# Attention's weights inverted in quarters of rows on 128 partitions, spread by DMA

## The chip, the cores and the metric

One core of a Trainium2 chip runs the whole kernel. The metric is the device time of one execution in microseconds (us), the median of several runs. One further execution was recorded by the profiler; every row below comes from it.

## The reference, cut to what matters

A macaron layer: half a feed-forward step, an attention-like mixer, half a feed-forward step. The batch is B = 4 sequences of T = 512 tokens and D = 512. The part that the change touches is the mixer's weights p_w and its normalisation; K = 32 heads of H = 8 channels, each with M = 8 phases.

```python
x = x + 0.5 * ffn(layernorm(x))            # top 2 of 8 experts, and a shared one
x = x + mixer(layernorm(x))                # the lines below
x = x + 0.5 * ffn(layernorm(x))            # the same weights

z = causal_conv4(layernorm(x) @ W_mem)     # in mixer: 256 values k_val, 32 scores s_raw
log_p = clip(score_scale * s_raw, -20, 20)
p_w = exp(log_p + log_w)                   # [b, l, K]
phi = k_val[..., None] * theta             # [b, l, K, H, M]
cs = cumsum([p_w, p_w * cos(phi), p_w * sin(phi)], axis=1)
den, num_re, num_im = split(cs)
inv_den = 1 / max(den, 0.0001)
state = (num_re + i num_im) * inv_den
out = sum over M of state * conj(q)        # q = x @ W_q
y = (y_val * silu(y_gate)) @ W_out         # from out, per head
```

## The kernel before, in words

All engines work from orders that a list planner writes when the program is built. `piece(engine, stage, cost, *after)` (L273 on) names a stage of a batch with its counted cost and what it comes after; `orders()` (L457) lets every engine in turn take the open piece with the longest way to the end, and the pieces of the phase steps on DVE yield to all others. On the chip each engine runs its list strictly in order, with semaphore waits. The planner's times are counts, the chip's are the trace's.

There are eight feed-forward jobs (four batches before attention, four after), each two a group: four groups of 23 blocks of expert rows, whose results are added to DRAM one block after another. Attention runs batch by batch between them: batches 0 and 1 when group 0 has been added, batches 2 and 3 when group 1 has. Jobs 4 and 5 read attention's batches 0 and 1, jobs 6 and 7 batches 2 and 3; group 3's blocks come last.

The head of attention's batch b (`plan_head`, L375):

- `a_mem` (PE, then DVE `convolve`, L1278): first the 32 rows of scores, then two tiles of k_val, 128 x 512 each.
- `a_p`: `log_weights` (L1292) on DVE, then `weights` (L1028) on ACT, the exp: p, 32 partitions (the heads) x 512 tokens, in `low_rows`.
- `a_fall`: `falls` (L1311), DVE: a reciprocal of p (L1316), then p of the token before times it (L1318). That is the factor by which the running sum falls from token to token, since the kernel scans sums already divided by p.
- `a_den`: `denominators` (L1320), DVE: a scan for the sums (L1324), the floor of 1e-4 (L1326), a reciprocal (L1328) and the fraction p / den (L1330), all 32 x 512. `s_row`, into which the scan writes, also holds the next batch's scores.
- `a_spread`: for each half, PE's `spread_falls` (L837) copies each head's row of falls to the head's 8 partitions by a matmul with a 0/1 matrix, and ACT's `keep_falls` (L1032) copies it from PSUM to `pwx`. Half 1 of `pwx` is read until the last scan of the batch before.
- `a_q`: four tiles of queries, which SP stores to DRAM (`store_query`, L1696).

Then 16 steps (`plan_step`, L413), n = 0 to 15, eight to a half. DVE makes the phases (`c_turn`, L1342 and L1344), ACT their sine and cosine (L1043 to L1046), DVE scans both (`c_scan`, L1355, reads `pwx`), multiplies them by the queries (`c_times`, L1362, L1367) and adds (`c_sum`, L1378 to L1388). SP loads the queries of a step (`load_query`, L1704) as soon as the step two before it has been summed. After step 7 and step 15 comes `c_out`: PE spreads the fractions (`spread_inverse`, L843), DVE scales (L1400), SP moves the result (`move_output`, L1718), and then the gates and the rows of the output follow on PE, ACT, DVE and POOL (`plan_tail`, L426).

DMAs of the head, the steps and the tail all are issued by SP, in one order. A job's input rows are fetched by SP too (`load_rows`, L1666); job 3's go into the buffer of batch 0's queries and wait for all four stores of them.

Of the kernel before, what the change touches and what calls it, by code (L numbers as in the profile page):

```python
# [9 lines left out]
F32 = mybir.dt.float32  # L10
# [5 lines left out]
P = 128  # L16
# [45 lines left out]
def macaron(nc, x, small, gate_w, sw1, sw2, b2_rows, w_experts, w_mem, w_q, w_bd, w_out, out):  # L62
# [32 lines left out]
    with ctx:  # L95
# [13 lines left out]
        pw, logw_sb = (low_rows[0:K, :, :], low_rows[2 * K:3 * K, :, :]), low_rows[K:2 * K, 0, :]  # L109
        w_all = sb("w_all", [P, E * WE])  # L110
# [121 lines left out]
        q_dram = nc.dram_tensor("q_cols", (2, KQ, M, HH, 2, T), F32)  # L232
        slots_dram = [nc.dram_tensor(f"slots{g}", (P * NB, 2), F32).ap() for g in range(NG)]
# [141 lines left out]
        def plan_head(b):  # L375
# [31 lines left out]
            for half in range(HALVES):  # L407
                s = ("a_spread", b, half)
                piece("PE", s, 1.2, ("DVE", ("a_fall", b)),
                      *([("DVE", ("c_scan", b - 1, half * M + M - 1))] if b else []), bank=[("misc", ("ACT", s))])  # L410
                piece("ACT", s, 0.6, ("PE", s))

        def plan_step(i):  # L413
# [6 lines left out]
            piece("DVE", ("c_scan", b, n), 2.5, ("ACT", ("c_turn", b, n)), ("ACT", ("a_spread", b, half)),  # L420
# [5 lines left out]
        def plan_tail(b):  # L426
# [3 lines left out]
            for half in range(HALVES):  # L430
# [5 lines left out]
                piece("PE", s, 1.3, ("DVE", ("a_den", b)), ("DVE", ("c_scan", b, half * M + M - 1)), *free,  # L436
# [123 lines left out]
        spread_p = signal("s_spread_p", staged("a_spread", "PE"))  # L560
# [19 lines left out]
        pwx_made = signal("s_pwx", staged("a_spread", "ACT"))  # L580
# [16 lines left out]
        den_made = signal("s_den", [(b, i) for b in range(B) for i in range(4)])  # L597
# [31 lines left out]
        a_loaded = [signal(f"s_a_loaded{tb}", range(B), 16) for tb in range(TB)]  # L629
        q_stored = [signal(f"s_q_stored{q}", range(B), 16) for q in range(KQ)]  # L630
# [24 lines left out]
        for s in ORDER:  # L655
# [24 lines left out]
            elif s[0] == "a_spread":  # L680
                misc_uses.append((s, pwx_made.at(s[1:])))
# [14 lines left out]
        def tensor_program():  # L696
# [140 lines left out]
            def spread_falls(b, half):  # L837
# [72 lines left out]
        def scalar_program():  # L910
# [121 lines left out]
            def keep_falls(b, half):  # L1032
                bank = misc_turn.at["a_spread", b, half][0]
                act.wait_ge(*spread_p.at((b, half)))
                if b > 0:
                    act.wait_ge(*scanned.at((b - 1, half * M + M - 1)))
# [839 lines left out]
```

## Time and profile before

| what | us |
|---|---|
| median of 3 runs | 1338.7 |
| lowest and highest | 1325.69, 1348.18 |
| the profiled execution, its own time | 1340.56 |
| its span, first to last instruction | 1339.3 |
| busy: PE, DVE, ACT, POOL | 1047.6, 731.5, 593.6, 439.6 |

The busy share of an engine is an average over stages with different limits, so the rows below go by stretch and by instruction. Times in rows are us from the span's start unless marked ns; PE is the tensor engine, DVE the vector engine, ACT the scalar engine, POOL GpSimd, SP the sync engine, and SPq its DMA queue.

### The profile page before, as it was taken

What the parts mean: (1) busy time and instruction counts of PE and PEld (TensorE: products, weight loads), DVE (VectorE), ACT (ScalarE), POOL (GpSimd) and SP (SyncE); (2) the same over time, 40 slices, a digit from 0 to 9 for tenths busy, and PEclk for the clock granted to TensorE, in tenths of its full rate; (3) what the DMA queues carried; (4) which work ended last, traced back from release to release, by engine and by line L of the source; (5) the groups of instructions that cost most, each with busy time, mean ns of one, the idle gap of its engine ahead of it and who ended that gap; (6) DMA issues with size and microseconds to landing.
All of it is one profiled execution on the core that took longest, in us unless ns stands there. A gap on an engine that the chain in (4) does not pass through costs nothing.

```text
span 1339.3 us, 10709 instructions
## 1 busy us (share of the span) xinstructions
PE 1047.6 (78%) x3296; PEld 574.9 (43%) x3296; DVE 731.5 (55%) x1130; ACT 593.6 (44%) x1008; POOL 439.6 (33%) x429
## 2 busy tenths in 40 slices
PE   5998888982978878968938287867977698969884
PEld 3545555332534444444313142344444443536552
DVE  3311000067879898979999885978988520200000
ACT  3423433233425888557323333357666541314332
POOL 4153443202553353331000246032452212154442
PEclk8998999995989989979968587989988899779887
DMA  8954554424144675773344624265685425034544
GB/s 284 332 171 87 94 95 79 79 58 134 36 98 109 173 143 117 160 196 93 94 111 87 206 56 93 60 179 112 134 215 108 68 37 112 32 64 95 94 85 56
DMA packets 60204, 155.15 MB, mean 116 GB/s; under 512 B 10578, under 2 KB 10578, under 8 KB 57974
## 3 DMA queue, kind: packets, MB, share of 16 engines
q0 software_dynamic: 29568, 60.90, 26.9%
q1 hardware_dynamic: 30582, 93.58, 22.6%
q8 instruction: 28, 0.46, 0.1%
q14 instruction: 26, 0.21, 0.1%
HBM read 99.74 MB, written 58.88 MB: 118 GB/s over the span
## 4 chain that ended last, share of the span: by engine, by line
DMA 33%; PE 27%; DVE 12%; POOL 10%; ACT 8%; issue 8%; SPq 1%; POOLq 0%; ACTq 0%; DVEq 0%
DMA x_rows<-ys,into_i 14%; DMA out_rows<-ys,into_i 10%; PE misc L867 6%; POOL slots L1538 6%; PE hps L736 5%; DMA xs<-x_normal,rows_i 4%; PE yps L805 3%; PE hps L789 3%; PE yps L748 2%; PE xps L719 2%; DVE run L1355 2%; ACT ys L975 2%; DMA xin<-in_x 1%; DMA xin<-x_rows 1%; ACT xin L996 1%
## 5 line engine op out<-in xcount | busy, mean ns | idle before, releaser
L805 PE MATMUL yps<-w_all,hidden_sb 128*128 x368 | 209.5, 700 | 55.8 <-ACT hidden_sb L962 55.0
L789 PE MATMUL hps<-w_all,hidden_sb 128*128 x736 | 188.2, 403 | 8.5 <-ACT hidden_sb L945 8.5
L1355 DVE TENSOR_TENSOR_SCAN run<-pwx,trig 128x512 f32<-128x512 f32 x128 | 149.5, 1210 | 46.0 <-ACT trig L1046 45.2
L789 PEld LDWEIGHTS hps<-w_all,hidden_sb 128*128 128x128 f32 x736 | 148.3, 207 | 54.3 <-issue 36.3
L1550 POOL DMA_INDIRECT xs<-x_normal,rows_i x92 | 106.1, 1153 | 139.2 <-PE xps L780 119.9
L975 ACT ACTIVATE ys<-yps,slots 128x512 f32<-128x512 f32 x92 | 63.1, 686 | 169.8 <-PE yps L805 62.3
L1563 POOL DMA_INDIRECT out_rows<-ys,into_i x46 | 77.5, 1685 | 166.5 <-ACT ys L975 94.2
L805 PEld LDWEIGHTS yps<-w_all,hidden_sb 128*128 128x128 f32 x368 | 74.3, 214 | 131.8 <-issue 129.8
L736 PE MATMUL hps<-xnT,sw_sb 128*128 128x512 f32 x256 | 129.9, 662 | 0.8 <-ACT xnT L919 0.8
L1563 POOL DMA_INDIRECT x_rows<-ys,into_i x46 | 77.8, 1691 | 153.9 <-DMA x_rows<-ys,into_i 85.0
L748 PE MATMUL yps<-sw_sb,hidden_sb 128*128 128x512 f32 x256 | 124.0, 629 | 0.0
L780 PE MATMUL xps<-ident,xs 128*128 128x128 f32 x368 | 59.9, 294 | 63.2 <-DMA xs<-x_normal,rows_i 54.8
L1538 POOL DMA_INDIRECT slots<-told,dest_i x64 | 79.7, 1245 | 64.6 <-DVE cmp_a L1225 32.5
L867 PE MATMUL misc<-turns_sb,tail_sb 128*128 128x512 f32 x192 | 88.8, 616 | 6.5 <-DVE tail_sb L1416 6.5
L710 PE MATMUL xps<-ident,xin 128*128 128x128 f32 x128 | 25.3, 353 | 74.8 <-ACT xin L996 68.8
L780 PEld LDWEIGHTS xps<-ident,xs 128*128 128x128 f32 x368 | 46.1, 151 | 83.3 <-DMA xs<-x_normal,rows_i 56.6
L736 PEld LDWEIGHTS hps<-xnT,sw_sb 128*128 128x128 f32 x256 | 53.3, 214 | 66.4 <-issue 65.9
L1362 DVE TENSOR_TENSOR trig<-run,qx 128x1024 f32<-128x1024 f32 x64 | 78.2, 1221 | 4.8 <-DMA qx<-q_cols 4.5
L1271 DVE BATCH_NORM_STATS2 stats_attn<-xin 128x6 f32<-128x512 f32 x16 | 10.5, 690 | 125.6 <-DMA xin<-x_rows 125.6
L1367 DVE TENSOR_TENSOR qx<-run,qx 128x1024 f32<-128x1024 f32 x64 | 78.0, 1219 | 0.0
L748 PEld LDWEIGHTS yps<-sw_sb,hidden_sb 128*128 128x128 f32 x256 | 48.2, 199 | 57.5 <-issue 57.5
L1043 ACT ACTIVATE trig<-trig 128x512 f32<-128x512 f32 x64 | 40.3, 630 | 71.1 <-DVE trig L1344 68.2
(199 smaller groups left out, 1587.4 us busy)
## 6 DMA issues: line engine op xcount, KB each, us to landing
qx<-q_cols SPq DMA_DIRECT2D x128, 256.0 KB
x_normal<-xin SPq DMA_DIRECT2D x32, 256.0 KB
w_all<-in_w_experts SPq DMA_DIRECT2D x8, 1024.0 KB, 8.3
xin<-x_rows SPq DMA_DIRECT2D x32, 256.0 KB, 4.7
turns_sb<-in_w_out SPq DMA_DIRECT2D x3, 1536.0 KB
xin<-in_x SPq DMA_DIRECT2D x16, 256.0 KB, 3.8
x_rows<-ys POOLq DMA_DIRECT2D x16, 256.0 KB
q_cols<-xin SPq DMA_DIRECT2D x16, 256.0 KB
```

The costliest lines, as they stand in the source:

```text
L736: t = PE.matmul(hps[:, bank, :], sw1_sb[:, c, n * P:(n + 1) * P], xnT[:, c, :], start=c == 0, stop=c == KC - 1)
L748: t = PE.matmul(yps[:, bank, :], hT[:, n, tb * P:(tb + 1) * P], sw2_sb[:, n, :], start=False, stop=n == SC - 1)
L780: t = PE.transpose(xps[:, bank, c * P:(c + 1) * P], xs[:, j % NX, c * P:(c + 1) * P], ident[:, :])
L789: t = PE.matmul(hps[:, bank, 0:H], xT[:, j % 2, c, :], w_all[:, bass.ds(expert[j] + c * H, H)], start=c == 0, stop=c == KC - 1)
L805: t = PE.matmul(yps[:, bank, :], hb[:, j % 2, ec, :], w_all[:, bass.ds(expert[j] + (KC * H + ec * D), D)], start=ec == 0, stop=ec == EC - 1)
L867: t = PE.matmul(misc[:, bank, :], yT[:, v, tb * P:(tb + 1) * P], wout_sb[:, v, :], start=v == 0, stop=v == VT - 1)
L975: SE.activation(ys[:, j % 2, :], yps[:, bank, :], ACT.Copy, scale=slots[:, g % 2, j, 1:2]).then_inc(*ys_kept.of((g, j)))
L1355: t = VE.tensor_tensor_scan(run[:, c, :], pwx[:, n // M, :], trig[:, n % 2, c, :], 0.0, ALU.mult, ALU.add)
L1362: VE.tensor_tensor(trig[:, n % 2, :, :], run[:, :, :], qx[:, n % NQX, :, :], ALU.mult).then_inc(*real_made.of((b, n)))
L1538: GE.indirect_dma_start(slots_dram[g], bass.IndirectOffsetOnAxis(dest_i[:, g % 2, t, r:r + 1], 0), told[:, g % 2, t, r, :], None).then_inc ...
L1550: GE.indirect_dma_start(xs[:, j % NX, :], None, xn_rows[g % 2], bass.IndirectOffsetOnAxis(rows_i[:, g % 2, j:j + 1], 0)).then_inc(*xs_load ...
L1563: GE.indirect_dma_start(INTO[g], bass.IndirectOffsetOnAxis(into_i[:, g % 2, j:j + 1], 0), ys[:, j % 2, :], None, compute_op=ALU.add).then_ ...
```

## The change

Falls and fractions are computed on all 128 partitions, each holding a quarter (128 tokens) of a head's row. ACT's exp still writes p on 32 partitions. SP stores p to DRAM, one element past the start of `u_dram`, and loads it back twice in quarters: from element 1 (`u_q`) and from element 0 (`fall_q`, the weights of the token before). DVE's `falls` works on these 128 x 128 tiles, SP stores the result, and one DMA for each half reads a head's row eight times over into `pwx`. The matmuls and the ACT copies of `a_spread` go. DVE scans the sums on 32 partitions as before, now straight after the exp; they make the same trip through DRAM, `fractions` works on quarters, and the result goes back through DRAM to `pw`. The planner counts these DMAs 2.4 us (2.8 for the spreads) past their issue. Cut to its core:

```diff
+        quarter_rows = sb("quarter_rows", [P, 3, T // 4])
+        u_q, fall_q, den_q = [quarter_rows[:, i, :] for i in range(3)]
...
                 free = [("DVE", ("c_turn", b - 2, i * M + M - 1))] if i < HALVES and b >= 2 else []
-                free += [("DVE", ("a_den", b - 1))] if i == HALVES and b else []
+                free += [("SP", ("a_den", b - 1, 0), 2.4)] if i == HALVES and b else []
                 piece("PE", s, 4.1, *kept_rows, weights, *free, *before, bank=[("misc", ("DVE", s))])
                 piece("DVE", s, 3.0, ("PE", s))
                 before = [("PE", s)]
             piece("DVE", ("a_p", b), 3.1, ("DVE", ("a_mem", b, HALVES)),
-                  *([("PE", ("c_out", b - 2, HALVES - 1)), ("PE", ("a_spread", b - 2, HALVES - 1))] if b >= 2 else []))
+                  *([("PE", ("c_out", b - 2, HALVES - 1))] if b >= 2 else []))
             piece("ACT", ("a_p", b), 0.7, ("DVE", ("a_p", b)), table="exp")
-            piece("DVE", ("a_fall", b), 4.0, ("ACT", ("a_p", b)))
-            piece("DVE", ("a_den", b), 5.8, ("DVE", ("a_fall", b)))
+            piece("SP", ("a_p", b, 0), 0.5, ("ACT", ("a_p", b)))
+            piece("SP", ("a_p", b, 1), 0.9, ("SP", ("a_p", b, 0), 2.4), *([("DVE", ("a_frac", b - 1))] if b else []))
+            piece("DVE", ("a_fall", b), 1.4, ("SP", ("a_p", b, 1), 2.4))
+            piece("SP", ("a_fall", b), 0.5, ("DVE", ("a_fall", b)))
+            piece("DVE", ("a_den", b), 1.4, ("ACT", ("a_p", b)))
+            piece("SP", ("a_den", b, 0), 0.5, ("DVE", ("a_den", b)))
+            piece("SP", ("a_den", b, 1), 0.5, ("SP", ("a_den", b, 0), 2.4))
+            piece("DVE", ("a_frac", b), 1.8, ("SP", ("a_den", b, 1), 2.4), ("SP", ("a_p", b, 1), 2.4))
+            piece("SP", ("a_frac", b, 0), 0.5, ("DVE", ("a_frac", b)))
+            piece("SP", ("a_frac", b, 1), 0.5, ("SP", ("a_frac", b, 0), 2.4))
...
                 s = ("a_spread", b, half)
-                piece("PE", s, 1.2, ("DVE", ("a_fall", b)),
-                      *([("DVE", ("c_scan", b - 1, half * M + M - 1))] if b else []), bank=[("misc", ("ACT", s))])
-                piece("ACT", s, 0.6, ("PE", s))
+                piece("SP", s, 0.5, ("SP", ("a_fall", b), 2.4),
+                      *([("DVE", ("c_scan", b - 1, half * M + M - 1))] if b else []))
...
-            piece("DVE", ("c_scan", b, n), 2.5, ("ACT", ("c_turn", b, n)), ("ACT", ("a_spread", b, half)),
+            piece("DVE", ("c_scan", b, n), 2.5, ("ACT", ("c_turn", b, n)), ("SP", ("a_spread", b, half), 2.8),
...
-                piece("PE", s, 1.3, ("DVE", ("a_den", b)), ("DVE", ("c_scan", b, half * M + M - 1)), *free,
+                piece("PE", s, 1.3, ("SP", ("a_frac", b, 1), 2.4), ("DVE", ("c_scan", b, half * M + M - 1)), *free,
...
             def falls(b):
-                p, fall = pw[b % 2][:, 0, :], pw[b % 2][:, 1, :]
+                vec.wait_ge(*u_loaded.at((b, 1)))
+                if b > 0:
+                    vec.wait_ge(*falls_stored.at(b - 1))
+                VE.reciprocal(den_q, u_q).then_inc(*falling.of((b, 0)))
+                vec.wait_ge(*falling.at((b, 0)))
+                VE.tensor_tensor(fall_q, fall_q, den_q, ALU.mult).then_inc(*falling.of((b, 1)))
+
+            def denominators(b):
+
+                none = zero1[b % 2 * 2 * K:(b % 2 * 2 + 1) * K, 0:1].broadcast_to([K, T])
                 vec.wait_ge(*p_made.at(b))
-                VE.reciprocal(fall, p).then_inc(*falling.of((b, 0)))
-                vec.wait_ge(*falling.at((b, 0)))
-                VE.tensor_tensor(fall[:, 1:T], p[:, 0:T - 1], fall[:, 1:T], ALU.mult).then_inc(*falling.of((b, 1)))
-
-            def denominators(b):
-
-                p, den = pw[b % 2][:, 0, :], s_row
-                none = zero1[b % 2 * 2 * K:(b % 2 * 2 + 1) * K, 0:1].broadcast_to([K, T])
-                VE.tensor_tensor_scan(den, p, none, 0.0, ALU.add, ALU.add).then_inc(*den_made.of((b, 0)))
-                vec.wait_ge(*den_made.at((b, 0)))
-                VE.tensor_scalar(den, den, 1e-4, None, ALU.max).then_inc(*den_made.of((b, 1)))
-                vec.wait_ge(*den_made.at((b, 1)))
-                VE.reciprocal(den, den).then_inc(*den_made.of((b, 2)))
-                vec.wait_ge(*den_made.at((b, 2)))
-                VE.tensor_tensor(p, p, den, ALU.mult).then_inc(*den_made.of((b, 3)))
-
-                vec.wait_ge(*den_made.at((b, 3)))
+                VE.tensor_tensor_scan(s_row, pw[b % 2][:, 0, :], none, 0.0, ALU.add, ALU.add).then_inc(*den_made.of(b))
+
+            def fractions(b):
+
+                vec.wait_ge(*den_loaded.at(b))
+                VE.tensor_scalar(den_q, den_q, 1e-4, None, ALU.max).then_inc(*part_made.of((b, 0)))
+                vec.wait_ge(*part_made.at((b, 0)))
+                VE.reciprocal(den_q, den_q).then_inc(*part_made.of((b, 1)))
+                vec.wait_ge(*part_made.at((b, 1)))
+                VE.tensor_tensor(den_q, u_q, den_q, ALU.mult).then_inc(*part_made.of((b, 2)))
...
-                vec.wait_ge(*pwx_made.at((b, n // M)))
+                vec.wait_ge(*falls_loaded[n // M].at(b))
...
+            def move_weights(b, part):
+                if part == 0:
+                    sp.wait_ge(*p_made.at(b))
+                    if b >= 2:
+                        sp.wait_ge(*u_loaded.at((b - 2, 1)))
+                    SP.dma_start(whole_rows(u_dram[b % 2], 1), pw[b % 2][:, 0, :]).then_inc(*u_stored.of(b))
+                else:
+                    sp.wait_ge(*u_stored.at(b))
+                    sp.wait_ge(*before_first.at(1))
+                    if b > 0:
+                        sp.wait_ge(*part_made.at((b - 1, 2)))
+                        sp.wait_ge(*falls_stored.at(b - 1))
+                    SP.dma_start(u_q, quarters(u_dram[b % 2], 1)).then_inc(*u_loaded.of((b, 0)))
+                    SP.dma_start(fall_q, quarters(u_dram[b % 2])).then_inc(*u_loaded.of((b, 1)))
+            def store_falls(b):
+                sp.wait_ge(*falling.at((b, 1)))
+                if b >= 2:
+                    for half in range(HALVES):
+                        sp.wait_ge(*falls_loaded[half].at(b - 2))
+                SP.dma_start(quarters(falls_dram[b % 2]), fall_q).then_inc(*falls_stored.of(b))
+            def spread_falls(b, half):
+                sp.wait_ge(*falls_stored.at(b))
+                if b > 0:
+                    sp.wait_ge(*scanned.at((b - 1, half * M + M - 1)))
+                src = bass.AP(falls_dram[b % 2].tensor, falls_dram[b % 2].offset + half * KT * T,
+                              [[T, KT], [0, HH], [1, T]])
+                SP.dma_start(pwx[:, half, :], src).then_inc(*falls_loaded[half].of(b))
+            def move_sums(b, part):
+                if part == 0:
+                    sp.wait_ge(*den_made.at(b))
+                    if b >= 2:
+                        sp.wait_ge(*den_loaded.at(b - 2))
+                    SP.dma_start(whole_rows(den_dram[b % 2]), s_row).then_inc(*den_stored.of(b))
+                else:
+                    sp.wait_ge(*den_stored.at(b))
+                    sp.wait_ge(*falling.at((b, 1)))
+                    SP.dma_start(den_q, quarters(den_dram[b % 2])).then_inc(*den_loaded.of(b))
+            def move_fractions(b, part):
+                if part == 0:
+                    sp.wait_ge(*part_made.at((b, 2)))
+                    if b >= 2:
+                        sp.wait_ge(*part_loaded.at(b - 2))
+                    SP.dma_start(quarters(part_dram[b % 2]), den_q).then_inc(*part_stored.of(b))
+                else:
+                    sp.wait_ge(*part_stored.at(b))
+                    sp.wait_ge(*den_made.at(b))
+                    sp.wait_ge(*u_stored.at(b))
+                    SP.dma_start(pw[b % 2][:, 0, :], whole_rows(part_dram[b % 2])).then_inc(*part_loaded.of(b))
...
+                    for i in range(2):
+                        SP.dma_start(u_dram[i][0:1, :], xs[0:1, i, 0:1]).then_inc(*before_first.of(i))
```

## Rows read from the trace of the kernel before

**Rows 1.** Busy time of each engine by stretch, with granted PE clock, DMA share, GB/s.

```profile
650.00:700.00 50.00, 27.06 (x61) 10.68 (x59) 48.72 (x56) 14.49 (x22) 2.59 (x3) 0.78 0.43 107
...
1250.00:1300.00 50.00, 42.60 (x158) 26.86 (x158) 0.00 (x0) 18.26 (x44) 21.93 (x17) 0.90 0.51 90
```

**Rows 2.** The chain that ended last, batch 2's head: start, us, what.

```profile
661.66 3.25 DVE low_rows L1316
...
669.60 3.35 DVE low_rows L1328
```

**Rows 3.** The same chain, batch 3's head.

```profile
849.17 3.35 DVE low_rows L1316
...
856.26 3.35 DVE low_rows L1328
...
861.80 1.21 PE misc L840 x2
...
872.35 7.51 DMA xs<-x_normal,rows_i
```

**Rows 4.** The same chain, batch 0's head.

```profile
287.45 3.26 DVE low_rows L1316
...
296.31 0.51 SPq L1701
...
296.86 14.10 DMA xin<-in_x
```

**Rows 5.** The same chain, batch 1's second spread.

```profile
509.84 1.05 PE misc L840 x2
```

**Rows 6.** DVE's groups by line and form: busy us, mean ns; idle before, releaser.

```profile
L1328 DVE RECIPROCAL low_rows<-low_rows 32x512 f32<-32x512 f32 x4 | 13.4, 3342 | 0.1
L1316 DVE RECIPROCAL low_rows<-low_rows 32x512 f32<-32x512 f32 x4 | 13.3, 3337 | 0.1
...
L1324 DVE TENSOR_TENSOR_SCAN low_rows<-low_rows,zero 32x512 f32<-32x512 f32 x4 | 4.9, 1214 | 0.1
...
L1330 DVE TENSOR_TENSOR low_rows<-low_rows 32x512 f32<-32x512 f32 x4 | 2.7, 680 | 0.1
...
L1326 DVE TENSOR_SCALAR low_rows<-low_rows 32x512 f32<-32x512 f32 x4 | 1.7, 416 | 0.1
...
L1161 DVE RECIPROCAL gr<-diff 128x4 f32<-128x4 f32 x8 | 1.4, 178 | 0.3
...
L1211 DVE TENSOR_TENSOR pair<-sel,dest 128x128 f32<-128x128 f32 x4 | 1.2, 293 | 0.1
```

**Rows 7.** DMA issues: count, KB each, median us from issue to landing.

```profile
xin<-x_rows SPq DMA_DIRECT2D x32, 256.0 KB, 4.7
...
slots<-slots SPq DMA_DIRECT2D x4, 23.0 KB, 3.4
```

**Rows 8.** The chain of waits: the last of four DMAs of `move_output`, batches 1 and 2.

```profile
696.35 3.65 DMA outT<-tail_sb
...
1000.11 8.30 DMA outT<-tail_sb
```

**Rows 9.** DVE in order of time: start, us, what, idle before.

```profile
301.43 2.34 DVE L1355 TENSOR_TENSOR_SCAN run<-pwx,trig 128x512 f32<-128x512 f32 x2
...
310.99 2.67 DVE L1110 BATCH_NORM_STATS2 stats_ffn<-xin 128x6 f32<-128x512 f32 x4 [3.78 <-DMA xin<-in_x]
...
362.19 2.33 DVE L1355 TENSOR_TENSOR_SCAN run<-pwx,trig 128x512 f32<-128x512 f32 x2
...
370.32 2.33 DVE L1355 TENSOR_TENSOR_SCAN run<-pwx,trig 128x512 f32<-128x512 f32 x2
```

**Rows 10.** ACT in order of time, batch 0's exp.

```profile
283.57 0.63 ACT L1030 ACTIVATE low_rows<-low_rows 32x512 f32<-32x512 f32 x1 [0.77 <-DVE low_rows L1309]
```

**Rows 11.** Who waited for whom: us in total, times, longest us.

```profile
DVE run L1355 <- ACT trig L1046: 45.2, 15, 6.1
```

**Rows 12.** The same of SP's queue.

```profile
SPq L1716 <- DVE outT L1388: 320.0, 39, 25.2
```

**Rows 13.** SP's queue in order of time, `load_tail_weights` of batch 1.

```profile
669.85 0.33 SPq L1734 DMA_DIRECT2D turns_sb<-in_w_out  x1
```

More of the change, by code:

```diff
@@ L232, in macaron, with quarters, whole_rows @@
         q_dram = nc.dram_tensor("q_cols", (2, KQ, M, HH, 2, T), F32)
+        u_dram = [nc.dram_tensor(f"weights{i}", (K * T + 1, 1), F32).ap() for i in range(2)]
+        falls_dram = [nc.dram_tensor(f"falls{i}", (K, T), F32).ap() for i in range(2)]
+        den_dram = [nc.dram_tensor(f"sums{i}", (K, T), F32).ap() for i in range(2)]
+        part_dram = [nc.dram_tensor(f"fractions{i}", (K, T), F32).ap() for i in range(2)]
+        def quarters(dram, start=0):
+            return bass.AP(dram.tensor, dram.offset + start, [[T // 4, P], [1, T // 4]])
+        def whole_rows(dram, start=0):
+            return bass.AP(dram.tensor, dram.offset + start, [[T, K], [1, T]])
         slots_dram = [nc.dram_tensor(f"slots{g}", (P * NB, 2), F32).ap() for g in range(NG)]
@@ L596, in macaron @@
         falling = signal("s_falling", [(b, i) for b in range(B) for i in range(2)])
-        den_made = signal("s_den", [(b, i) for b in range(B) for i in range(4)])
+        den_made = signal("s_den", range(B))
+        part_made = signal("s_part", [(b, i) for b in range(B) for i in range(3)])
         phase_int = signal("s_phase_int", staged("c_turn", "DVE"))
@@ L629, in macaron @@
         a_loaded = [signal(f"s_a_loaded{tb}", range(B), 16) for tb in range(TB)]
+        u_stored = signal("s_u_stored", range(B), 16)
+        u_loaded = signal("s_u_loaded", [(b, i) for b in range(B) for i in range(2)], 16)
+        falls_stored = signal("s_falls_stored", range(B), 16)
+        falls_loaded = [signal(f"s_falls_loaded{half}", range(B), 16) for half in range(HALVES)]
+        den_stored = signal("s_den_stored", range(B), 16)
+        den_loaded = signal("s_den_loaded", range(B), 16)
+        part_stored = signal("s_part_stored", range(B), 16)
+        part_loaded = signal("s_part_loaded", range(B), 16)
+        before_first = signal("s_before_first", range(2), 16)
         q_stored = [signal(f"s_q_stored{q}", range(B), 16) for q in range(KQ)]
@@ L1030, in weights @@
                 SE.activation(pw[b % 2][:, 0, :], pw[b % 2][:, 0, :], ACT.Exp).then_inc(*p_made.of(b))
[L1032 to L1036, printed above, removed]
-                SE.copy(pwx[:, half, :], misc[:, bank, :]).then_inc(*pwx_made.of((b, half)))
             def waves(b, n):
@@ L1285, in convolve @@
                     vec.wait_ge(*phase_made.at((b - 2, i * M + M - 1)))
+                if i == HALVES and b:
+                    vec.wait_ge(*den_stored.at(b - 1))
                 VE.tensor_scalar(o, z, conv_sb[at, i, CW - 1:CW], None, ALU.mult).then_inc(*convolved.of((b, i, 0)))
@@ L1480, in vector_program @@
                     denominators(*at)
+                elif stage == "a_frac":
+                    fractions(*at)
                 elif stage == "c_turn":
@@ L1786, in sync_program @@
                     store_query(*at)
+                elif stage == "a_p":
+                    move_weights(*at)
+                elif stage == "a_fall":
+                    store_falls(*at)
+                elif stage == "a_spread":
+                    spread_falls(*at)
+                elif stage == "a_den":
+                    move_sums(*at)
+                elif stage == "a_frac":
+                    move_fractions(*at)
                 elif stage == "c_query":
```

17 lines of the change are left out of this document (1 added, 16 removed).

## The prediction

> **What bounds the kernel now.** I read the busy times by stretch first. Ahead of attention and behind it DVE stands still (0 of 50 us at 1250 [rows 1]) and the adding of expert blocks sets the time; between some 300 and 1060 us DVE is the engine that is nearly full (48.7 of 50 us at 650 [rows 1]). Averages over the span (DVE 55%) hide that. Then the chain of waits, which shows where the head of a batch is on the path. Batch 2: both reciprocals on the chain [rows 2]. Batch 3: both again, behind them the two matmuls of a spread (1.21 us), and through PE's order the next block's rows [rows 3]. Batch 0: the falls' reciprocal, which holds up the first phases, through them the query tile that ACT copies behind their sines, its store, and job 3's rows [rows 4]. Batch 1: of its head only a spread [rows 5]; its arithmetic is beside the path, since blocks of group 1 set the pace there. Last the waits: DVE loses 45.2 us at 15 scans to ACT's late sines [rows 11], so a DVE that is faster elsewhere partly waits there instead.
>
> **DVE's work.** Before, a batch costs 3.34 + 3.34 (reciprocals) + 2 x 0.68 (multiplies) + 1.21 (scan) + 0.42 (floor) = 9.67 us [rows 6]. A reciprocal takes 3342 ns at 512 elements a partition and 178 at 4, so 6.23 ns an element, whether on 32 or 128 partitions; at 128 elements that gives 178 + 124 x 6.23 = 950 ns. A multiply of 128 x 128 stands in the rows (0.29) [rows 6]. The floor is between 0.18 and 0.29; I take 0.24. After: 2 x 0.95 + 2 x 0.29 + 1.21 + 0.24 = 3.93 us. The gain is 5.74 us a batch, 23 us of DVE's work in all; on the path only for batches 2 and 3.
>
> **PE and ACT.** 16 matmuls (8 spreads) and 8 ACT copies go. On the path stand 1.21 us for batch 3 and 1.05 us for batch 1 [rows 3, 5]; I count these 2.26 us as won, the rest at nothing, as DVE's or the blocks' waits cover it.
>
> **The new round trips.** No row shows a 64 KB DMA through DRAM. Call L the time from issue to landing. From below: 3.4 us for 23 KB [rows 7]. From above: 8.3 us, the slower of two moves of 128 KB within SBUF; the other took 3.65 [rows 8]. I take 3.65, which is nearest to the small DMAs' median, and keep 3.4 and 8.3 for the range. An issue costs SP some 0.55 us (0.51 in [rows 4]).
>
> The exp to `falls`: store (0.55 + L), then two loads (1.1 + L): 2L + 1.65 = 8.95 us. DVE's order is fixed, so `falls` waits there with all phase steps queued behind it, for whatever the planner has not filled. It counts this trip 0.1 + 0.5 + 2.5 + 0.9 + 2.5 = 6.5 us and lets DVE finish a piece of up to 2.5. A step that it counts 9.1 (1.3 + 2.5 + 2.5 + 2.8) takes 8.13 us, from scan to scan [rows 9], so this cover is worth 0.89 of its count: 5.8 us, with half a piece 6.9. A stall of 2.05 us is left.
>
> The sums to `fractions`: the load waits for `falling`, since `den_q` is the falls' scratch, but the planner doesn't list that wait. It may put `fractions` right behind `falls`, or one piece later. The load takes 0.55 + 3.65 = 4.2 us behind the falls; between no cover and 2.3 us of it I take the middle, 1.15: a stall of some 3.05 us. Together the stalls are 3L - 5.85, or 5.1 us a batch against 5.74 won; they are equal at L = 3.86 us.
>
> The way of the falls into `pwx` (one store, two spreads) and of the fractions back (two DMAs) has cover. Batch b's first scan comes many steps after its head for b = 1 to 3, and the fractions are read after step 7, seven steps of 8.13 us later. SP gets ten more DMAs a batch (some 5.5 us) with four waits for landings between them. Its queue stood idle for 320 us waiting for DVE's sums before it could load queries [rows 12]; a load is wanted one step after it may go, so holding SP up by some 4 us (8.13 less an issue pair and a landing of 3 to 4) costs nothing, two trips in a row would. I cost that at 0 and keep it in the slow rival. Two 4-byte stores at the start lie beside the first weights' loads: 0.
>
> The Trainium skill, "DMA: Bandwidth & Descriptors", section "Anatomy of one DMA — SWDGE (gpsimd) path", fits a DMA at about 2.0 us plus bytes over 436 GB/s. By it a 64 KB trip would be an estimated 2.15 us (this queue is another than the one it was fitted on), the stalls 0.6 us a batch and the sum near the fast rival; the 3.4 us row stands against it.
>
> **Batch 0.** The exp ends at 284.20 [rows 10]. Quarters loaded at 293.15, falls at 294.4, stored at 298.6, spread (256 KB, 4.7 us [rows 7]) at 303.85: the first scan is 2.4 us later than the 301.43 of before, less than the 3.78 us that DVE idled just after for job 3's rows [rows 9]. Against it the first phases start up to 3.9 us earlier (reciprocal and multiply gone from ahead of them), and job 3's rows with them, if SP isn't holding for falls just then; the falls' store lands 2.3 us after the 296.31 at which the last query store went [rows 4]. Between -3.9 and +2.4 I take -1.
>
> **Sum.** Batch 0 -1; batch 1 -1.05; batch 2 5.1 - 5.74 = -0.6; batch 3 the same and -1.21, -1.8. Together -4.5 us on the profiled execution's 1340.56, 1336.1. That execution is 1.86 above the median of the runs shown; so 1334 us, to compare with 1338.7. The arithmetic is won, and nearly all of it given back as waits for landings.
>
> **The rivals.**
> 1. The trips are covered, as the planner means them to be. The whole 5.74 comes through twice, batch 0 gives 3.9, the spreads 2.26: -17.6, or 1321 us. For it: DVE's pieces come in lumps, and a stall at `falls` lets ACT catch up on sines it would have been waited for anyway (45.2 us [rows 11]). Against it: 3.4 us is the shortest landing in the rows, and the planner counts 2.4. The skill's fit, above, would give this case.
> 2. Small DMAs land late, behind larger ones on SP's queue. The place is DVE's two in-order waits. At L = 8.3 each batch stalls 19.05, +13.3 for batch 2 and +12.1 for batch 3; batch 0's first scan slips by four trips x 4.65 = 18.6 more, less the idle left, +17; with batch 1, +41, or 1380 us. It decides from L = 3.86, and passes 2% slower near L = 6.9. For it: query loads of 2 x 256 KB and a load of 1.5 MB at 669.85 [rows 13] are issued by SP within 10 us of batch 2's head. Against it: only one of the moves seen took that long.
>    The skill, same page, section "Queues, rings and completion order", says that each DMA engine takes descriptors in ring order. By this a small DMA stands behind the query loads ahead of it; the 3.65 and the 8.3 agree with it without showing it.
> 3. The orders of all engines are planned anew, since costs and pieces changed. That moves blocks, sines and table loads against one another without anything in the change meaning it. Half of the 45.2 us of waits for sines gained or lost is 22 us either way: 1312 or 1356.
> 4. It doesn't take DVE's time down: a reciprocal on 128 partitions costs by some other count. The equal per-element rate of 32 x 512 and of 128 x 4 speaks against it; with no gain and these stalls, +8: 1348. Small.
>
> **How the numbers follow.** Forecast 0.5, own range 1325 to 1346. Rival 1 0.17, rival 2 0.13, rival 3 0.17, rival 4 0.03. The range is 1312 to 1364: below, rival 3's fast end beyond rival 1; above, rival 2 up to L of about 6.8. A measurement of this kernel tells 2%, 27 us, from no change (below 1312, above 1365). Faster by that needs rival 1 and luck of order together: 0.10. Slower needs rival 2 well past its point, or a bad order with stalls: 0.16. Within: 0.74.
>
> **What would show it.** Right: reciprocals of 128 x 128 at 0.9 to 1.0 us; DVE's busy time down by 23 us; idle ahead of the falls' reciprocal and of the floor on quarters, released by DMAs from `weights` and `sums`, some 20 us in all over four batches; batch 0's first scan at 302 to 306. Wrong: no idle there and a span below 1325 (rival 1); over 8 us idle at either in a batch, or scans waiting for queries (rival 2); the stalls as told but blocks and sines in other places with tens of us between them (rival 3).

## The result, and the profile after

The changed kernel takes 1328.25 us (median of 18 runs, 1318.9 to 1340.46) against 1336.69 us for the kernel before on the same chips (18 runs, 1325.69 to 1348.18): ratio 0.9929, 95% interval 0.9904 to 0.9954. By the medians that is 8.4 us faster, clear of the noise and well within 2%. A ratio is estimated from the single runs, so it can differ from the quotient of the two medians, here by up to 0.3%. The forecast was 1334 us, 4.5 us of gain, with a range of 1312 to 1364. The profiled execution has a span of 1325.1 us against 1339.3.

First the engines' busy times, from the page of the changed kernel.

```profile
PE 1021.4 (77%) x3280; PEld 564.0 (43%) x3280; DVE 708.5 (53%) x1130; ACT 594.9 (45%) x1005; POOL 448.8 (34%) x429
```

DVE's busy time is down by 23.0 us from 731.5. The groups by line and form show the same instructions on quarters, to be held against [rows 6]:

```profile
L1343 DVE RECIPROCAL quarter_rows<-quarter_rows 128x128 f32<-128x128 f32 x4 | 3.8, 952 | 0.1
L1328 DVE RECIPROCAL quarter_rows<-quarter_rows 128x128 f32<-128x128 f32 x4 | 3.8, 950 | 11.4 <-DMA quarter_rows<-weights 11.4
...
L1330 DVE TENSOR_TENSOR quarter_rows<-quarter_rows 128x128 f32<-128x128 f32 x4 | 1.2, 292 | 0.1
...
L1341 DVE TENSOR_SCALAR quarter_rows<-quarter_rows 128x128 f32<-128x128 f32 x4 | 0.9, 226 | 7.6 <-DMA quarter_rows<-sums 7.6
```

Read the part behind the bar (busy us, mean ns of one; idle us just before, with what ended it): the falls' reciprocal (L1328) stood 11.4 us waiting for its quarters, the floor (L1341) 7.6 us for the sums. Of 23 us of work won, 19.0 us come back as waits. The four batches differ; DVE in order of time, batches 0 and 1:

```profile
299.05 0.95 DVE L1328 RECIPROCAL quarter_rows<-quarter_rows 128x128 f32<-128x128 f32 x1 [10.12 <-DMA quarter_rows<-weights]
...
304.37 0.23 DVE L1341 TENSOR_SCALAR quarter_rows<-quarter_rows 128x128 f32<-128x128 f32 x1 [1.03 <-DMA quarter_rows<-sums]
...
394.70 0.95 DVE L1328 RECIPROCAL quarter_rows<-quarter_rows 128x128 f32<-128x128 f32 x1 [0.69 <-DMA quarter_rows<-weights]
...
400.18 0.23 DVE L1341 TENSOR_SCALAR quarter_rows<-quarter_rows 128x128 f32<-128x128 f32 x1 [4.20 <-DMA quarter_rows<-sums]
```

Batch 2 waits 0 and 1.89 us, batch 3 0.62 and 0.49. These are not DVE's only new waits. Over the whole span, the changed kernel's multiplies wait 11.2 us for loads of queries, against 4.5 before, while its scans wait 27.5 us for sines, against 45.2 [rows 11]:

```profile
DVE run L1368 <- ACT trig L1059: 27.5, 12, 8.5
...
DVE trig L1375 <- DMA qx<-q_cols: 11.2, 2, 6.5
```

The queries' wait of before:

```profile
DVE trig L1362 <- DMA qx<-q_cols: 4.5, 2, 3.8
```

So where does the 14.2 us between the two profiled executions come from? Instructions that both traces have cut the span into stretches. A first sum is DVE's first addition of a half's first step (`c_sum`, steps 0 and 8), a scaling is its `scale_output`, behind steps 7 and 15:

| stretch | before | after | difference |
|---|---|---|---|
| start to attention's first rows | 250.83 | 249.53 | -1.3 |
| from there to the first sum of batch 3's step 8 | 733.80 | 736.97 | +3.2 |
| from there to the scaling after step 15 | 81.89 | 67.73 | -14.2 |
| from there to the end | 272.8 | 270.9 | -1.9 |

All four heads, with all that the change touches, lie in the second stretch, and there the changed kernel is not faster. How far to trust the rows: in a second trace of the changed kernel, the run e_after_again below, the second stretch takes 746.9 us and the third 67.7. So the +3.2 is less than two executions of one kernel differ by, and the -14.2 is far more. The gain is in batch 3's last eight steps, in which DVE has the same work as before. Busy times of that stretch (us: PE, PEld, DVE, ACT, POOL, granted PE clock, DMA share, GB/s), before and after:

```profile
984.63:1066.52 81.89, 57.75 (x181) 34.05 (x182) 59.05 (x76) 51.94 (x87) 24.94 (x23) 0.83 0.53 109
```

```profile
986.50:1054.23 67.73, 51.26 (x175) 30.77 (x174) 58.96 (x76) 51.03 (x83) 28.93 (x21) 0.90 0.58 126
```

DVE runs the same 76 instructions in 59.0 us in both. Who kept it waiting in that stretch (us in total, times, longest us), before and then after:

```profile
DVE run L1355 <- ACT trig L1046: 16.2, 4, 6.1
DVE tail_sb L1412 <- ACT tail_sb L1056: 4.2, 2, 2.4
DVE tail_sb L1400 <- PE misc L846: 2.1, 1, 2.1
```

```profile
DVE run L1368 <- ACT trig L1059: 4.6, 1, 4.6
DVE tail_sb L1425 <- ACT tail_sb L1069: 2.2, 2, 1.3
DVE tail_sb L1413 <- PE misc L868: 1.5, 1, 1.5
```

DVE waits 22.5 us before and 8.3 after: the 14.2 us. PE's granted clock is 0.90 after against 0.83, each a mean between its two levels of 1.2 and 2.4 GHz; PE stood idle for 16.5 us of the stretch after, for 24.1 before. The shorter stretch comes with the higher clock; no run separates the two. The planner has put the block work of group 2 and the sines in another order. One more wait there is ACT's. It copies each block's rows into one of two `ys` buffers, and must wait until the add of the block two before has landed in DRAM:

```profile
ACT ys L975 <- DMA out_rows<-ys,into_i: 14.3, 4, 6.2
```

That is before; after, ACT has no such wait in the stretch. So rival 3 has to be tested against the forecast's own reasons.

### The profile page after: what moved, and what is told of

It is laid out like the page before. It is cut to its first block, busy times and chain, and to the rows that moved or that the text cites. A ratio compares the mean times of both kernels' runs of the same rounds, so it can differ in the third digit from the quotient of the medians.

```text
span 1325.1 us, 10725 instructions
## 1 busy us (share of the span) xinstructions
PE 1021.4 (77%) x3280; PEld 564.0 (43%) x3280; DVE 708.5 (53%) x1130; ACT 594.9 (45%) x1005; POOL 448.8 (34%) x429
## 4 chain that ended last, share of the span: by engine, by line
DMA 35%; PE 26%; ACT 11%; POOL 10%; DVE 10%; issue 8%; SPq 1%; POOLq 0%; ACTq 0%; DVEq 0%
DMA x_rows<-ys,into_i 12%; DMA out_rows<-ys,into_i 10%; POOL slots L1553 6%; PE hps L764 5%; PE misc L889 4%; DMA xs<-x_normal,rows_i 4%; PE yps L833 4%; PE hps L817 3%; DMA xin<-x_rows 2%; PE xps L747 2%; DVE run L1368 2%; ACT ys L995 2%; PE misc L852 2%; PE yps L776 2%; ACT L982 1%
## 5 line engine op out<-in xcount | busy, mean ns | idle before, releaser
L833 PE MATMUL yps<-w_all,hidden_sb 128*128 x368 | 191.2, 646 | 49.5 <-ACT hidden_sb L982 48.8
L817 PE MATMUL hps<-w_all,hidden_sb 128*128 x736 | 192.2, 409 | 9.4 <-ACT hidden_sb L965 9.1
L1368 DVE TENSOR_TENSOR_SCAN run<-pwx,trig 128x512 f32<-128x512 f32 x128 | 149.3, 1207 | 30.2 <-ACT trig L1059 27.5
L1578 POOL DMA_INDIRECT out_rows<-ys,into_i x46 | 80.7, 1754 | 155.6 <-ACT ys L995 73.9
L1578 POOL DMA_INDIRECT x_rows<-ys,into_i x46 | 80.6, 1752 | 151.8 <-DMA x_rows<-ys,into_i 93.4
L833 PEld LDWEIGHTS yps<-w_all,hidden_sb 128*128 128x128 f32 x368 | 70.3, 202 | 118.8 <-issue 116.5
L776 PE MATMUL yps<-sw_sb,hidden_sb 128*128 128x512 f32 x256 | 120.0, 612 | 0.0
L1553 POOL DMA_INDIRECT slots<-told,dest_i x64 | 76.2, 1191 | 72.8 <-DVE cmp_a L1236 37.8
L889 PE MATMUL misc<-turns_sb,tail_sb 128*128 128x512 f32 x192 | 92.4, 637 | 10.7 <-DVE tail_sb L1429 10.7
L1375 DVE TENSOR_TENSOR trig<-run,qx 128x1024 f32<-128x1024 f32 x64 | 78.0, 1219 | 11.4 <-DMA qx<-q_cols 11.2
```

The lines of the kernel that those rows point to most:

```text
L776: t = PE.matmul(yps[:, bank, :], hT[:, n, tb * P:(tb + 1) * P], sw2_sb[:, n, :], start=False, stop=n == SC - 1)
L817: t = PE.matmul(hps[:, bank, 0:H], xT[:, j % 2, c, :], w_all[:, bass.ds(expert[j] + c * H, H)], start=c == 0, stop=c == KC - 1)
L833: t = PE.matmul(yps[:, bank, :], hb[:, j % 2, ec, :], w_all[:, bass.ds(expert[j] + (KC * H + ec * D), D)], start=ec == 0, stop=ec == EC - 1)
L889: t = PE.matmul(misc[:, bank, :], yT[:, v, tb * P:(tb + 1) * P], wout_sb[:, v, :], start=v == 0, stop=v == VT - 1)
L1368: t = VE.tensor_tensor_scan(run[:, c, :], pwx[:, n // M, :], trig[:, n % 2, c, :], 0.0, ALU.mult, ALU.add)
L1375: VE.tensor_tensor(trig[:, n % 2, :, :], run[:, :, :], qx[:, n % NQX, :, :], ALU.mult).then_inc(*real_made.of((b, n)))
```

## The experiments

Theory A is the forecast's: DVE's arithmetic in the heads is on the path, and is mostly given back as waits for landings. Theory B is rival 3: the gain is the order that the planner wrote for the new pieces. The experiments fall into three groups, on chips 14, 10 and 14. Each ratio is to the kernel before in the same group (medians 1336.73, 1330.06 and 1340.77 us).

**Less arithmetic, old order.** The kernel before, with falls and fractions cut to 128 of 512 columns. The rest of the falls is left at zero (a tile `short`), so its output is another one:

```diff
-                VE.reciprocal(fall, p).then_inc(*falling.of((b, 0)))
+                VE.reciprocal(fall[:, 1:P + 1], p[:, 1:P + 1]).then_inc(*falling.of((b, 0)))
...
-                VE.reciprocal(den, den).then_inc(*den_made.of((b, 2)))
+                VE.reciprocal(den[:, 0:P], den[:, 0:P]).then_inc(*den_made.of((b, 2)))
```

> The kernel before, in its own order and with PE's spreads, but the falls' reciprocal and multiply and the fractions' floor, reciprocal and multiply work on 128 of 512 columns (falls are 0 for the other tokens, and the falls' tile stands in for the fractions in the second spread, so the mixer's output is another one). DVE loses 5.7 us a batch, nothing waits for a trip. Theory A (arithmetic on the path): batches 2 and 3 give 5.7 each and batch 0 up to 3.9, so 11 to 15 us faster than before, ratio 0.989 to 0.992. Theory B (the gain is the new order, the arithmetic is covered): within 4 us of before, ratio 0.997 to 1.0.

Measured: 1331.52 us, ratio 0.9966 (0.9937 to 0.9995), just below Theory B's range and well short of Theory A's. Its trace says where. From attention's first rows to the first sum of batch 3's step 8 it takes 726.1 us against 733.8, 7.7 less. Cut at the first sum of each half of a batch, the stretch that holds batch 2's head takes 95.7 us and batch 3's 109.6. Three traces of the old work in the old order up to there (the kernel before, and the runs e_late_order and e_sines_ahead below) have 101.2 to 102.8 and 115.7 to 116.8. So these two are some 6 us shorter, where the cut removes 5.8 us of DVE each. Batch 1's is not shorter (123.7 against 121.4 to 123.1). The last eight steps take 85.7 us instead of 81.9. In the old order the arithmetic reaches the path where Theory A has it, but only some 5 us of it are left at the end of the kernel.

**The arithmetic back, new order.** The changed kernel with spare reciprocals behind each wait:

```diff
+                vec.wait_ge(*spared.at(4 * b + 0))
+                VE.reciprocal(spare[:, 0:200], spare[:, 0:200]).then_inc(*spared.of(4 * b + 1))
...
                 VE.reciprocal(den_q, u_q).then_inc(*falling.of((b, 0)))
```

> The changed kernel in its own order; inside `falls` two more reciprocals of 128 x 200 and inside `fractions` two of 128 x 215, behind the waits, so that DVE has its 5.7 us a batch back. Theory A: 11 us slower than the changed kernel for batches 2 and 3, so ratio to before 0.999 to 1.003. Theory B: at most 4 us slower than the changed kernel, ratio 0.993 to 0.996.

Measured: 1345.47 us, ratio 1.0065 (1.0033 to 1.0097), 1.4% slower than the changed kernel by the two ratios: 18 us (13 to 24, by the intervals) for 23 us of DVE work. That is outside both ranges, and more than Theory A's 11. Where the time goes is not shown. Three traces have the changed work in the new order up to batch 3's step 8 (the changed kernel twice, and e_late_old below), and take 737.0, 743.9 and 746.9 us from attention's first rows to there; with the spare work it is 757.8. The stretch with batch 1's head takes 120.8 us against 115.3 to 120.0, batch 2's 112.7 against 109.5 to 113.6, batch 3's 114.6 against 108.3 to 115.2. Each lies within 1 us of the longest of the three. The one that stands out holds no head: from batch 1's first sum to that of its step 8, 91.4 us against 84.5 to 86.9.

**The two orders exchanged.** In both kernels the planner's lists were replaced after planning. Here is the edit that puts the changed kernel's work in the old order, shortened and with comments added:

```diff
-        ORDERS = orders()
+        ORDERS, ENDED = orders()          # with the plan of before
+        ORDERS = old_order()              # the new pieces put in by time
```

> The changed kernel's work, but PE, ACT, DVE, POOL and SP keep the order of the kernel before for all that both have; the sums' scan stands where the falls stood, the falls where the denominators stood, the fractions a step later, the new DMAs of SP between by time. Theory A: about the changed kernel's time or some us less, since the falls have more cover, ratio 0.989 to 0.994. Theory B: as the kernel before, ratio 0.998 to 1.002.

> The kernel before's work (32 partitions, PE's spreads), in the order that the changed kernel's planner writes; the old denominators stand where the fractions stand, the spreads on PE and ACT go in by time. Theory A: no faster than before, ratio 0.998 to 1.003 (1334 to 1341 us). Theory B: as the changed kernel, ratio 0.991 to 0.995.

Measured, with the two kernels themselves, as ratios:

| | old order | new order |
|---|---|---|
| old work | 1 | 0.9928 (0.9897 to 0.9958) |
| new work | 1.0119 (1.0071 to 1.0167) | 0.9929 (0.9904 to 0.9954) |

The old arithmetic on 32 partitions, with PE's spreads, gains in the new order just what the changed kernel gains. Theory B holds: in one and the same order, the new work and the old differ by 0 us, give or take 5. In the old order the new work costs 1.2%, which neither theory had. The order written by hand around it has less cover, as DVE's waits of that kernel show:

```profile
DVE quarter_rows L1359 <- DMA quarter_rows<-sums: 24.4, 4, 9.5
```

Another 13.9 us go to the weights: 38.3 us of waits against 19.0. So part of that 1.2% is likely my placing of the new pieces, not the old order as such.

The kernel with the old work in the new order also shows what the new DMAs do to the queries. Without them, DVE's waits over the whole span are:

```profile
DVE run L1386 <- ACT trig L1077: 40.6, 14, 9.5
...
DVE trig L1393 <- DMA qx<-q_cols: 0.2, 1, 0.2
```

With the new work, in the same order, the queries' wait is 11.2 us and the sines' 27.5. So the changed kernel wins 23 us of DVE's work and 13 us of waits for sines, and pays 19 us at the trips, 11 us for late queries and 2 us at batch 0's first scan (waits of one trace each). That is some 4 us, and the two kernels' times are equal within 5.

**Only the late order.** The plan of before for what it starts ahead of batch 3's step 8, the plan of after from there:

```diff
+        limit = ENDED["DVE", ("c_scan", 3, 8)] - 2.5
+        for engine, stages in ORDERS.items():
+            early = [k for k in stages if ENDED[engine, k] - old_work[engine, k][0] < limit]
+            late = [k for k in later[engine] if k not in early and (engine, k) in old_work]
+            ORDERS[engine] = early + late
```

> The kernel before's work; every engine keeps the order of before for what the plan starts ahead of the scan of batch 3's step 8, and from there on takes the order of the changed kernel's plan. Theory B1 (the gain is the order of the last eight steps and the output of batch 3): as fast as the whole new order, ratio 0.990 to 0.994, with some 68 us from step 8's first sum to the second scaling instead of 82. Theory B2 (the new order gains all along): half the gain or less, ratio 0.996 to 1.0.

Measured: 0.9901 (0.9867 to 0.9936), in Theory B1's range. Its last eight steps, in busy times by stretch:

```profile
980.41:1048.24 67.83, 52.08 (x175) 31.65 (x176) 58.88 (x76) 51.22 (x84) 29.26 (x22) 0.90 0.57 128
```

And the reverse on the changed kernel, beside the changed kernel itself:

> The changed kernel's work and its own order up to the scan of batch 3's step 8, and from there on the order of the kernel before. If the order of the last eight steps is where the changed kernel's gain comes from, it loses all of it: some 82 us instead of 68 from step 8's first sum to the second scaling, ratio 0.999 to 1.006. If the arithmetic or the order ahead of it brings the gain, ratio 0.991 to 0.996.

> The changed kernel itself, as the reference of this chip for the three below: ratio 0.990 to 0.995.

Measured: 1.0023 (0.9996 to 1.0051) with the old late order, 0.9914 (0.9882 to 0.9946) for the changed kernel on that chip.

```profile
995.72:1076.72 81.00, 55.56 (x180) 32.60 (x178) 59.02 (x75) 51.33 (x85) 26.21 (x23) 0.83 0.53 108
```

Either kernel takes 68 us with the new late order and 81 to 82 with the old, and has the gain or doesn't. This is shown from both sides. In all traces of this case, the eight with the new late order take 65.7 to 69.0 us there, the four with the old one 81.0 to 85.7.

**A plan that differs for no reason.** One number of the planner in the kernel before:

```diff
-        HOP = 0.1
+        HOP = 0.15
```

> The kernel before with one number of the planner changed (the step between engines counted 0.15 us instead of 0.1), so the same work in an order that differs about as much as the changed kernel's does, meant for nothing. If any new order moves the time by a per cent either way (theory B), the ratio lies outside 0.996 to 1.004, on either side. If orders of this kind are worth little (theory A), it lies within.

Measured: 0.9936 (0.9907 to 0.9964). A new plan meant for nothing is worth about as much as the change. Its last eight steps take 77.4 us, 4.5 less than before, so the rest of its gain comes from elsewhere.

**What in the late order.** ACT's list alone, in the kernel before:

```diff
+        line = ORDERS["ACT"]
+        for n in (10, 11, 14, 15):
+            i = line.index(("c_turn", 3, n))
+            while line[i - 1][0] in ("one", "x", "two", "turn", "norm"):
+                line[i - 1], line[i] = line[i], line[i - 1]
+                i -= 1
```

> The kernel before, in its own order but for ACT's list: the sines of batch 3's steps 10, 11, 14 and 15 move ahead of the block copies and of job 6's normalisation that stand directly before them. If the late order gains because ACT no longer stands waiting for an add or for POOL with the next sines behind it, DVE's waits for sines in the last eight steps go from 16 us to under 8 and the ratio is 0.991 to 0.996. If it is something else in the order (PE's), the ratio is 0.997 to 1.002.

Measured: 1.0000 (0.9969 to 1.0032), so it is something else in the order. DVE's waits in its last eight steps:

```profile
DVE tail_sb L1418 <- ACT tail_sb L1062: 11.7, 2, 9.9
DVE tail_sb L1406 <- PE misc L852: 9.5, 1, 9.5
DVE run L1361 <- ACT trig L1052: 3.3, 3, 1.8
DVE tail_sb L1421 <- ACT tail_sb L1065: 0.9, 1, 0.9
```

The sines' wait fell from 16.2 to 3.3 us as meant. Two other waits took its place: a gate of batch 3's first half (9.9 us in one wait), and at the very end the scaling, 9.5 us, since PE's spread of the fractions stands in PE's list behind a block's matmuls. The stretch takes 84.6 us. Sines that come late were where it showed, not what set the pace.

The traces point at the adds of the blocks. ACT's wait for them is still there in this kernel:

```profile
ACT ys L981 <- DMA out_rows<-ys,into_i: 9.0, 3, 5.2
```

In the last eight steps ACT waits 14.3 to 17.4 us for adds in the four traces with the whole old late order, 9.0 in this one, 10.4 with the hop of 0.15 us, and not at all in the eight with the new late order. In the first six the chain that ended last runs through five or six adds there, in the eight through none. No run changed the adds' place alone, so this cause is argued from the traces, not shown; which entries of PE's, ACT's and POOL's late lists make the 14 us stays open.

**The wait that the planner doesn't list.** The changed kernel with a tile of its own for the falls' reciprocal:

```diff
-                VE.reciprocal(den_q, u_q).then_inc(*falling.of((b, 0)))
+                VE.reciprocal(turned_q, u_q).then_inc(*falling.of((b, 0)))
...
                     sp.wait_ge(*den_stored.at(b))
-                    sp.wait_ge(*falling.at((b, 1)))
+                    if b > 0:
+                        sp.wait_ge(*part_stored.at(b - 1))
```

> The changed kernel, in its own order; the falls' reciprocal has a tile of its own, so SP loads the sums in quarters without waiting for the falls. The wait of the floor for the sums, 7.6 us over four batches in the changed kernel's trace, goes to under 2. Theory A (DVE's time ahead of the fractions is on the path for batches 2 and 3): 2 to 5 us faster than the changed kernel, ratio 0.989 to 0.992. Theory B: the same time as the changed kernel, within 2 us.

Measured: 0.9851 (0.9796 to 0.9906), some 0.8% better than the changed kernel by the ratios (their intervals touch), and more than either theory had. The floor's row:

```profile
L1341 DVE TENSOR_SCALAR quarter_rows<-quarter_rows 128x128 f32<-128x128 f32 x4 | 0.9, 223 | 0.9 <-DMA quarter_rows<-sums 0.9
```

The wait for the sums fell from 7.6 to 0.9 us. The gain is some 10 us by the two ratios. Two more kernels with the same edit, below, have 0.9859 and 0.9851; the second of them, beside the changed kernel's 0.9914 in its group, is 5 us (medians) to 8 us (ratios) faster. So the gain is there in three kernels and about as large as the 6.7 us of waits; its exact size isn't settled. These are the fastest forms found, 1.2% under the kernel before by the medians and 1.5% by the ratios, in the order that the changed kernel has anyway.

**Batch 0's trip.** In the changed kernel SP stores batch 0's weights late, behind a query load. SP in order of time, changed kernel:

```profile
279.26 0.54 SPq L1716 DMA_DIRECT2D q_cols<-xin  x1
287.29 1.31 SPq L1786 DMA_DIRECT2D qx<-q_cols  x2
289.06 0.34 SPq L1725 DMA_DIRECT2D weights<-low_rows  x1
289.46 1.22 SPq L1786 DMA_DIRECT2D qx<-q_cols  x2
294.82 0.33 SPq L1732 DMA_DIRECT2D quarter_rows<-weights  x1
```

The exp ended at 281.94, but SP waited for the queries' store to land before its query load at 287.29, and the weights' store stands behind that. Two attempts on top of the own scratch, the store ahead of the query load, then all four DMAs of weights and sums:

```diff
+        line = ORDERS["SP"]
+        head = [("a_p", 0, 0), ("a_p", 0, 1), ("a_den", 0, 0), ("a_den", 0, 1)]
+        for k in head:
+            line.remove(k)
+        i = line.index(("c_query", 0, 0))
+        line[i:i] = head
```

> The same, and batch 0's weights are stored ahead of the first query loads in SP's order, which in the changed kernel's trace held the store up for some 6 us. The falls of batch 0 wait some 4 us instead of 10, first scan at 302 instead of 308. Theory A: 4 us more than the own scratch alone, ratio 0.986 to 0.990, if batch 0's head is on the path; the same as the own scratch alone, if job 3's rows set the pace there.

> The changed kernel with a tile of its own for the falls' reciprocal, and batch 0's store and loads of weights and sums all ahead of the first query load in SP's order. With only the store ahead the loads still stood behind the query loads, and those behind the queries' stores. DVE's wait for batch 0's weights goes from 9 us to some 3, its first scan comes some 5 us earlier. If batch 0's head is on the path: 3 to 5 us faster than the own scratch alone, ratio 0.981 to 0.984; if not, the same as it, 0.985.

Measured: 0.9859 (0.9806 to 0.9913) and 0.9851 (0.9802 to 0.9900), no more than the own scratch alone. With the store alone ahead, the loads still stood behind the queries, batch 0's wait stayed at 8.7 us, and the first scan came 24.2 us after the exp (25.1 with the own scratch alone). With all ahead, the wait fell to 1.13, and the next trip took the time instead:

```profile
290.52 0.95 DVE L1334 RECIPROCAL quarter_rows<-quarter_rows 128x128 f32<-128x128 f32 x1 [1.13 <-DMA quarter_rows<-weights]
...
310.62 2.34 DVE L1374 TENSOR_TENSOR_SCAN run<-pwx,trig 128x512 f32<-128x512 f32 x2 [14.36 <-DMA pwx<-falls]
```

```profile
291.21 2.60 SPq L1793 DMA_DIRECT2D qx<-q_cols  x4
293.85 0.55 SPq L1722 DMA_DIRECT2D q_cols<-xin  x1
294.44 2.04 SPq L1746 DMA_DIRECT2D falls<-quarter_rows  x1
307.25 1.21 SPq L1755 DMA_DIRECT2D pwx<-falls  x2
```

The first scan comes at 310.62, which is 28.2 us after the exp, later than in any other form. Whether an earlier first scan would be worth anything was therefore not tested.

## Why the prediction was right

The time lay inside the range and on the forecast side, but the account behind it did not come out. Step by step:

- **DVE's work** came out as worked: reciprocals at 950 and 952 ns (950), multiplies at 292 (0.29), the floor at 0.23 (0.24), 23.0 us in all (23). The rate of 6.23 ns an element, from which it was worked, holds at two more lengths: the spare reciprocals of 200 and 215 elements took 1403 and 1500 ns, worked out 1399 and 1493.
- **The waits in DVE's order.** Forecast 5.1 us a batch, some 20 in all; measured 19.0 in all, 11.4 at the falls and 7.6 at the sums. The total was right and its spread was not: batch 0 alone takes 11.2, batch 1 4.9, batches 2 and 3 1.9 and 1.1. The planner's cover was better than I took it where other steps run, and missing where none do. The wait for `falling` that the planner doesn't list was real: own scratch removed 6.7 us of waits and about as much time.
- **SP's being held up, counted at nothing,** was not nothing. The forecast let SP be late by some 4 us for free. For batches 2 and 3 SP waited 8.6 and 8.2 us for the falls' store to land, with a load of weights and the next queries behind it, and DVE's waits for queries came to 11.2 us, against 0.2 in the same order without the new DMAs. That the new DMAs cost these waits is shown by that exchange; that they do it by holding up SP's line is argued from its order. The sum has no such term.
- **"On the path only for batches 2 and 3"** did not carry over. In the old order it holds: the short form wins nothing in batch 1. But the changed kernel runs in the new order, and there spare work of the same size costs 18 of 23 us, where two batches would account for 11.5. Which other part of it is on the path the traces don't show. The reading came from one chain of one order, and the order moved.
- **Batch 0, -1 us**, was mis-sized. From the exp's end to the first scan there are 26.0 us (281.94 to 307.92), where the forecast had 19.65 and the kernel before 17.2. I started the store when the exp ended; SP's order had it behind a query load, which waits for a landing. I didn't ask what held up the new DMAs themselves.
- **The sum.** Up to batch 3's step 8 the forecast's terms apply: -4.5 forecast (with all of the spreads), +1.9 measured from the start, +3.2 from attention's first rows. There the arithmetic is won and given back, as said, and with it more that was not in the sum. Batch 0 is the surest part: 69.5 us from the first rows to its first sum in both traces of the changed kernel, 65.4 before. The total is not sure to the microsecond, since the second trace is 10 us longer in that stretch.
- **Rival 3** had a chance of 0.17, with 22 us either way. It is what happened: -14.2 us in the last eight steps of the profiled pair, in work that the change doesn't touch. The forecast was near the result by luck: the changed work is worth nothing net (give or take 5 us) and the new order some 9 us. Its own gains did not come through.

Rival 1 failed (19 us of waits), though one thing said for it was so: a DVE that waits at the trips waits less for sines. Rival 2 came in part: two stores of falls took 8.3 and 9.5 us to land behind query loads (below), not at DVE's two waits but in SP's line, ahead of a load of weights and the next queries. Rival 4 failed by the 950 ns.

## What to carry to other kernels

When a list planner writes every engine's order, a change to its costs or pieces is two changes. Time the new order with the old work (or a plan perturbed for nothing) before crediting the edit: here a hop counted 0.15 instead of 0.1 us was worth 0.6%, about as much as the edit. Profile one kernel twice before reading a difference of a few us in a stretch: here one stretch differed by 10 us between two executions, and another by 0.1. A resource shared for convenience, a scratch tile here, is a dependency; list it in the plan or remove it (here 6.7 us of waits, where all the arithmetic took 23 us off DVE). And a trip through DRAM off an engine pays only if the issuing queue is free when it starts: look at what stands ahead of each new DMA in its queue, and at what it holds up behind it, not at its own length.

## What the runs showed of the hardware

A 64 KB store can land very late behind larger DMAs of the same queue, in the changed kernel too. Its DMAs through DRAM, all 64 KB (count, KB each, median us from issue to landing):

```profile
quarter_rows<-weights SPq DMA_DIRECT2D x8, 64.0 KB, 2.7
weights<-low_rows SPq DMA_DIRECT2D x4, 64.0 KB, 3.6
...
falls<-quarter_rows SPq DMA_DIRECT2D x4, 64.0 KB, 9.2
```

Batch 0's falls were issued at 300.76 (0.43 us) with no query load right ahead, and their store had landed by 304.56, 3.4 us on. Batch 2's stood right behind a store and two loads of queries, 256 KB each, and landed 9.5 us after its issue; batch 3's, in the same place, 8.3 us after:

```profile
671.41 0.52 SPq L1716 DMA_DIRECT2D q_cols<-xin  x1
671.98 1.51 SPq L1786 DMA_DIRECT2D qx<-q_cols  x2
673.59 0.39 SPq L1740 DMA_DIRECT2D falls<-quarter_rows  x1
...
683.45 0.57 SPq L1749 DMA_DIRECT2D pwx<-falls  x1
```

In the last experiment, with four query loads (issued 291.21 to 293.81) and a query store (293.85) right ahead of it, batch 0's store ended its issue at 296.48 and had landed by 307.25, 10.8 us on. The forecast's upper bound was 8.3. This agrees with the ring order that the Trainium skill states ("DMA: Bandwidth & Descriptors", "Queues, rings and completion order": each DMA engine takes its descriptors in ring order), though no run here separates it from plain shared bandwidth.

The Trainium skill's fit on the same page ("Anatomy of one DMA — SWDGE (gpsimd) path"), 2.0 us and bytes over 436 GB/s, fitted on another queue, gives an estimated 2.15 us for 64 KB. Batch 1's weights show about that: their store's issue ended at 389.04 and their loads began at 391.38, 2.3 us on. Batch 0's weights took longer, 5.4 us from 289.40 to 294.82.

A reciprocal's time goes by the elements of a partition, not by the partitions. It took 178 ns at 4 elements, 950 at 128, 1403 at 200 and 1500 at 215, all on 128 partitions, and 3342 at 512 on 32: some 6.2 ns for each further element throughout.
